# Moving GpSimd's router steps and norm roots, two pair masks, and the order of the last expert products in a fused attention and expert kernel

## The reference, cut to what matters

```
x = x + L0_xattn(layernorm(x), ctx, ...)      # windowed attention-free mixer, then a 512-wide MLP
x = x + L0_ffn(layernorm(x), ...)             # quantised gated MLP
x = x + L1_xattn(layernorm(x), ctx, mask)     # 16 heads of 8 channels, softmax over 256 keys
x = x + L1_ffn(layernorm(x), ...)             # 8 experts, each token sent to one of them
```

```
wg_n   = wg / max(norm(wg), 1e-4)
logits = (x @ w_red) @ wg_n.T                 # 8 logits a token
idx, score = argmax, max of softmax(logits)
h = gelu(x @ W1[idx] + b1[idx])               # 128 -> 256
o = (h @ W2[idx] + b2[idx]) * score           # 256 -> 128
```

## Time and profile before

| | us |
|---|---|
| median of 3 runs | 244.88 (243.72 to 244.91) |
| the profiled execution | 242.69 |
| its span, first to last instruction | 240.9 |
| TensorE busy | 189.6 |
| VectorE busy | 175.1 |
| ScalarE busy | 135.0 |
| GpSimd busy | 112.0 |

### The profile page before, as it was taken

How to read it: one execution, slowest core, us unless ns; L and a number is a source line. 1 busy time by engine, 2 the same in 40 slices (tenths; PEclk the granted TensorE clock), 3 DMA queues, 4 the chain that set the end, 5 groups by cost and what they waited for, 6 DMA issues and landing times.

```text
span 240.9 us, 4754 instructions
## 1 busy us (share of the span) xinstructions
PE 189.6 (79%) x1750; PEld 136.1 (56%) x1750; DVE 175.1 (73%) x455; ACT 135.0 (56%) x271; POOL 112.0 (47%) x205
## 2 busy tenths in 40 slices
PE   0489865998584948766979988987978885899993
PEld 0368644888341748652434534534636774798883
DVE  4678889899889587869857796886566565749252
ACT  2236755929885638435767668768792347350200
POOL 8131677994497057831587885785040031000000
PEclk9999999999978579999999999999999999999999
DMA  5996040000000000000000000000000000000000
GB/s 168 345 369 257 0 155 24 0 3 0 1 3 0 0 0 3 3 3 0 3 1 4 0 3 1 0 3 0 3 1 3 0 1 3 0 3 22 24 22 22
DMA packets 4461, 8.75 MB, mean 36 GB/s; under 512 B 514, under 2 KB 3026, under 8 KB 4052
## 3 DMA queue, kind: packets, MB, share of 16 engines
q1 hardware_dynamic: 3636, 7.78, 8.8%
q10 hardware_dynamic: 800, 0.63, 0.9%
HBM read 7.89 MB, written 0.52 MB: 35 GB/s over the span
## 4 chain that ended last, share of the span: by engine, by line
PE 30%; DVE 25%; POOL 18%; issue 11%; ACT 10%; DMA 2%; SPq 1%; POOLq 0%; DVEq 0%; ACTq 0%
PE ps L1364 26%; POOL gate_pt L541 6%; PE ps L1373 5%; POOL w L431 3%; POOL rstd L410 2%; DMA wf<-weights_dram 2%; DVE stats L851 2%; DVE hid_xm L1010 2%; POOL spread L528 2%; DVE amax L1085 2%; DVE ka_mem L1051 1%; DVE mx L1202 1%; ACT gate_pt L811 1%; POOL vareps L407 1%; DVE moments L857 1%
## 5 line engine op out<-in xcount | busy, mean ns | idle before, releaser
L1202 DVE TENSOR_REDUCE mx<-ps 128x2 f32<-128x512 f32 x64 | 41.9, 686 | 13.8 <-PE ps L1364 13.5
L811 ACT ACTIVATE gate_pt<-ps 128x512 f32<-128x512 f32 x64 | 36.6, 603 | 9.7 <-PE ps L1364 9.6
L1364 PE MATMUL ps<-w,hid_xm 128*128 128x256 f16 (+1 forms) x288 | 28.7, 255 | 0.5 <-DVE hid_xm L1010 0.5
L541 POOL TENSOR_SCALAR gate_pt<-ka_mem 32x256 f16<-32x256 f16 x64 | 25.5, 398 | 4.4 <-issue 0.2
L1364 PE MATMUL ps<-gate_pt,half_c 128*128 128x512 f16 x64 | 24.2, 380 | 3.3 <-issue 1.9
L1364 PEld LDWEIGHTS ps<-w,hid_xm 128*128 128x128 f16 x288 | 24.5, 98 | 2.9 <-POOL w L423 0.7
L1364 PE MATMUL ps<-qb,gate_pt 128*128 128x256 f16 x128 | 24.7, 275 | 0.2 <-ACT gate_pt L811 0.2
L1364 PE MATMUL ps<-gate_pt,hid_xm 128*32 128x256 f32 x256 | 20.2, 390 | 0.9 <-ACT gate_pt L811 0.9
L1364 PEld LDWEIGHTS ps<-qb,gate_pt 128*128 128x128 f16 x128 | 9.8, 97 | 14.9 <-issue 8.8
L410 POOL TENSOR_TENSOR rstd<-vareps,halfs 128x2 f32<-128x2 f32 (+1 forms) x19 | 15.8, 833 | 1.6
L528 POOL TENSOR_SCALAR spread<-mx 128x16 f16<-128x16 f32 x32 | 5.9, 203 | 21.5 <-DVE mx L1202 16.1
(11 more groups left out here) (222 smaller groups left out, 510.4 us busy)
## 6 DMA issues: line engine op xcount, KB each, us to landing
stage<-weights_dram SPq DMA_DIRECT2D x2, 1024.0 KB, 11.1
wf<-weights_dram SPq DMA_DIRECT2D x4, 256.0 KB, 8.6
wf<-mask_dram SPq DMA_DIRECT2D x1, 1024.0 KB, 4.8
eb_oT<-ffw_dram SPq DMA_DIRECT2D x1, 768.0 KB, 8.0
ctx_in<-ctx_rows_dram ACTq DMA_DIRECT2D x4, 128.0 KB, 5.5
x_in<-x_dram SPq DMA_DIRECT2D x4, 128.0 KB, 3.2
gate_pt<-ctx_cols_dram SPq DMA_DIRECT2D x1, 512.0 KB, 8.5
out_dram<-ctx_in SPq DMA_DIRECT2D x4, 128.0 KB, 1.7
```

The costliest lines, as they stand in the source:

```text
L541: ins = nc.gpsimd.tensor_scalar(kz[part, n % KRING, k], ka[part, b, quad], 1.0, 0.0, ALU.mult, ALU.add)
L811: nc_act(pt[:, head % PRING].rearrange("p t n -> p (t n)"), ps[:, 2 + head % 2, :], ACT.Exp, scale=DK ** -0.5).then_inc(sig["probs"], 1)
L1202: V.tensor_reduce(mx[:, b, head:head + 2, t], score_bank(4 * n + i).rearrange("p (h n) -> p h n", h=2), AX.X, ALU.max).then_inc(sig["smax" ...
L1364: return nc.tensor.matmul(dst, lhsT, rhs, start=start, stop=stop, skip_group_check=True)
```

## The change

It has four parts.

1. POOL's six router steps move from the first three rounds of the attention loop to the place between the first copies of the keys and `shift_rows(0)`.
2. POOL's roots for batches 0 and 1 move from the head of rounds 7 and 11 to rounds 6 and 10, behind `shift_rows` and `separated_keys` of the round and ahead of its quarter of a low part.
3. On DVE `pair_masks(0)` and `pair_masks(1)` move behind the two divisions (`tail_dve(3, 0)` and `(3, 1)`) of batch 3. On ACT `tail_rows(3)` moves behind `onehot_copy(2, 1)` and `gelu(1)`.
4. On TensorE `outputs(0, 0)` moves ahead of `tail_step(3, 4)`, `hidden(2, 0)` ahead of `tail_step(3, 5)`, and `outputs(0, 1)` from behind `onehot_columns(3, 1)` to ahead of `tail_step(3, 6)`.

No instruction is added or removed.

```diff
-POOL_ROOTS = (7, 11)
+POOL_ROOTS = (6, 10)
...
             pool.wait_ge(sig["kz_ready"], KRING)
+            for step in range(6):
+                router_part(step)
             shift_rows(0)
             shift_rows(1)
             for n in range(B * QUADS):
-                if n in POOL_ROOTS:
-                    rstd_of(LN_MOE, POOL_ROOTS.index(n))
-                    rows_shift(LN_MOE, POOL_ROOTS.index(n))
                 if n + 2 < B * QUADS:
                     shift_rows(n + 2)
                 if n + KRING < B * QUADS:
                     pool.wait_ge(sig["spread"], n + 3)
                     separated_keys(n + KRING)
                     pool.wait_ge(sig["kz_ready"], n + KRING + 1)
-                if n < 3:
-                    router_part(2 * n)
-                    router_part(2 * n + 1)
+                if n in POOL_ROOTS:
+                    rstd_of(LN_MOE, POOL_ROOTS.index(n))
+                    rows_shift(LN_MOE, POOL_ROOTS.index(n))
                 if n in M1_AT:
                     split_lo_quarter("m1", 9, M1_AT.index(n))
...
             onehot_copy(2, 0)
             gelu(0)
-            tail_rows(3)
             onehot_copy(2, 1)
             gelu(1)
+            tail_rows(3)
             tail_act(3, 4)
...
             masked_tokens(1)
-            pair_masks(0)
-            pair_masks(1)
             tail_dve(3, 0)
             tail_dve(2, 5)
             tail_dve(3, 1)
+            pair_masks(0)
+            pair_masks(1)
             gates(0)
...
             pe.wait_ge(sig["w_lo_pool"], 14)
+            outputs(0, 0)
             tail_step(3, 4)
-            outputs(0, 0)
+            hidden(2, 0)
             tail_step(3, 5)
-            hidden(2, 0)
+            outputs(0, 1)
             tail_step(3, 6)
             onehot_columns(3, 0)
             hidden(2, 1)
             onehot_columns(3, 1)
-            outputs(0, 1)
             outputs(1, 0)
```

## The result

The changed kernel took 237.8 us (median of 4 runs, 236.81 to 238.3) against 244.3 us (4 runs) for the kernel before: a ratio of 0.9725, 95% interval 0.9674 to 0.9776. Forecast were 236.7 us and a range of 235.0 to 239.4. In a second comparison it took 236.16 us against 244.07, a ratio of 0.967 (0.9615 to 0.9726), which is 7.9 us. A ratio is estimated over the runs of both kernels and is not quite that of the two medians. Each term of the prediction came out within 0.3 us.

A forecast was written before the change was run, and what follows sets the result against it. No engine was taken as the bound throughout; TensorE's waits for others were priced place by place. Gains of 1.9 + 2.2 + 4.0 = 8.1 us, taken from the median of 244.88, gave 236.7 us, range 235.0 to 239.4.

The forecast's parts named there:

- The last split of the chances: Whole kernel: faster by more than 1.2 us 92%, 1 of it given to the middle; within 4%; slower 5%.
- Router steps, 1.9 us: POOL, early loop: spread 1.04 us earlier plus 0.88 us shorter distance; steps free with 1.0 us to spare.
- The rhythm without them: Attention loop on TensorE: shift products 3.35 us apart where no router step of weight lies between.
- One sign of being wrong: POOL at the loop's start: the forecast is wrong if the first spread comes later than 110.4 us.
- Roots, 2.2 us: Loop, batches 0 and 1: POOL's root, ACT's rows and TensorE's step 4 each 1.12 us earlier; ends 0 and 3.0 us.
- That tie: POOL's earlier root in the loop: its wait for DVE's moments was taken as 0.0 us long.
- The 0.1 us that the spread of quad 9 was given to spare: Loop: POOL's next spread done at about 144.9 us, TensorE reaching its shift at about 145.0.
- Masks, 1.1 us: Behind the loop: batch 3's division ends at about 186.0 us and TensorE goes straight on, gaining 1.1 us.
- Orders, 2.9 us: Behind the loop on TensorE: wait of 2.83 us becomes 1.0, 1.8 less, and step 5's 1.10 us wait goes.
- The lock between POOL and DVE: Batch 3's root behind the loop: POOL starved beside DVE, rows 0.6 to 2.1 us late, 237.3 to 238.8 us; 15%.
- The loss of 0.6 us that the prediction had by the rule alone: Batch 3's root behind the loop: by the exclusive-lock rule alone the summed gain would be 0.6 us smaller.
- The slower rival, TensorE's clock: New waits at 182 to 209 us lower the clock over the last 28 us; at half, 251 us; 4%.

The follow-up runs named there:

- the two kernels with early fillers: Changed kernel plus unread TensorE products ahead of gated_turned(2) and in quad 1, without or with low-part quarters and step 4 moved later: 234.99 and 233.56 us.
- the repetition: The changed kernel run again beside the kernel before on the same chip: 236.16 us, ratio 0.967.
- The three more powers: Changed kernel with three extra unused powers of 128x8 values on POOL behind the router steps, ahead of shift_rows(0): 239.69 us, ratio 0.9801 to the kernel before.

## Why the prediction was right

- **The bound and the sum.** 8.1 us were summed up, and the trace has 1.76 + 2.06 + 4.25 = 8.1. That the sums agree to the tenth is luck: parts 1 and 2 brought 0.3 us less than their terms, parts 3 and 4 0.25 more. The first comparison showed 6.5 us, the second 7.9; both medians lie in the range. The forecast's 236.7 (its own terms give 236.8) was 1.1 us low in the first. The scatter of the runs was put at half a per cent and is larger, and TensorE's clock ahead of the change has a part in it: one execution of the same instructions lost 3.0 us there. The last split of the chances is a point off both ways: by its own list 5% lie within 1.2 us of no change and 4% are slower.
- **Router steps, 1.9 us.** Measured 1.76. The rhythm without them is 3.40 us and not 3.35, the one distance that I had taken. The steps took 4.6 us of a 5.3 us gap: free, with 0.6 us left, where 1.0 was expected. In the two kernels with early fillers the spread followed the steps after 0.17 us, or with no wait shown: there the slack is all but gone. One sign of being wrong came up by its letter, a first spread later than 110.4 us (113.28), but that spread waited for DVE's maxima, in an execution that was 3.0 us late, and stood at 110.15 in the repetition. The three more powers show where that ends.
- **Roots, 2.2 us.** Measured 2.06. Once earlier, POOL was there 0.18 us before DVE's moments. That tie had been read off, and priced at nothing. The 0.1 us that the spread of quad 9 was given to spare were 0.12.
- **Masks, 1.1 us.** Measured 1.21 by undoing them.
- **Orders, 2.9 us.** With the masks 4.0 were forecast and 4.25 measured. Waits of 0, 1.0, 0 and 0.56 us became 0, 1.08, 0 and 0.55. The 0.2 us more is what an idle row leaves out: it counts from the modelled end of one product, and starts are what adds up.
- **The lock between POOL and DVE.** The mechanism is there: one more of POOL's operations was stretched, from 0.19 to 0.55 us. It cost nothing, as forecast, since 0.8 us of slack were left. The root in two phases was not blocked twice (1.56 us against 1.57 before). This also agrees with the exclusive lock of the Trainium skill (SBUF — State Buffer, "SBUF: two separate sides"), if a whole root is held up once: it ran from 196.60 to 198.16 us, across the start of one DVE instruction (197.52), and 1.56 - 0.70 = 0.86 us of that is delay. The loss of 0.6 us that the prediction had by the rule alone did not come.
- **The slower rival, TensorE's clock.** It was expected behind the loop and as the change's harm. In the changed kernel's two traces the clock is 1.00 there. It fell behind long waits of the old orders: to 0.50 behind 3.18 us and behind 2.83 us of waiting, in two kernels. But it stayed at 1.00 behind the same 2.83 us in the one trace of the kernel before, so the wait alone doesn't decide it. Behind 1.08 and 1.85 us it never fell. What the rival left out is the start of the loop, where the clock did fall and cost 0.5 to 1.0 us, with the change or without part 1.

## What to carry to other kernels

Price an edit by the start-to-start distances on the engine that it should free, and check it by the same distances: where the clock was 1.00 (B, C, D) they repeated to 0.01 us from one execution to the next, while two medians of the same changed kernel differed by 1.6 us, nearly what the smallest part was worth. Work of an engine off the path is free only as far as its idle gap reaches, and the gap can shrink when another engine gets faster. Orders on three engines that feed each other are to be changed together: TensorE's alone undone cost 3.80 of the 4.44 us, 1.7 of them by the clock.

## What the runs showed of the hardware

TensorE's clock moved the time by as much as a part of the change did. With the same instructions up to 104 us, the first `shift` started at 111.45 in one execution and at 114.44 in another, with granted clocks of 1.00 and 0.83 at 30 to 60 us, 0.67 and 0.80 at 80 to 90, and 0.98 and 0.88 at 90 to 104. The dip at the loop's start cost 0.5 to 1.0 us (A of 6.03 to 6.55 us instead of 5.5). With products that nobody reads at the start of the loop the clock was 1.00 there in both traces (A of 5.50 and 5.51 us), and in only one of the twelve without them. Put into the wait of 2.83 us they gave 1.00 behind it, where it had been 0.50 in one kernel and 1.00 in another. They paid at the loop's start, where TensorE was the bound, and not behind the other wait, where it ran into another engine's lateness.
